# Both cross attentions: scores and row maxima two and a half units ahead in place of three, and the split of the maxima at the end of GpSimd's turn

## The reference, cut to what matters

```
scores = q k^T * scale            # 512 x 512 a head
p      = softmax(scores, axis=-1)
out    = p v                      # channels x 512
x      = layernorm(x + project(out))   # the second one has no projection
```

## Time and profile before

| | us |
|---|---|
| median of three runs | 3492.27 |
| lowest and highest | 3489.34, 3504.04 |
| the profiled execution's own time | 3488.51 |
| its span, first to last instruction | 3486.6 |
| c0, first row maximum to the last normalized batch | 525.67 to 943 |
| c1, the same | 2249.07 to 2932 |
| granted clock of PE, mean of the span | 0.939 |

### The profile page before, as it was taken

How to read it: one execution, slowest core, us unless ns; L and a number is a source line. 1 busy time by engine, 2 the same in 40 slices (tenths; PEclk the granted TensorE clock), 3 DMA queues, 4 the chain that set the end, 5 groups by cost and what they waited for, 6 DMA issues and landing times. The chain is left out here.

```text
span 3486.6 us, 57867 instructions
## 1 busy us (share of the span) xinstructions
PE 3037.0 (87%) x21948; PEld 1766.3 (51%) x21948; DVE 2121.2 (61%) x2636; ACT 1542.6 (44%) x2674; POOL 929.9 (27%) x1329
## 2 busy tenths in 40 slices
PE   7999968999579958999996999589999995889997
PEld 4444323333256636888885676222222222767785
DVE  4555658999335543444444344699999992572167
ACT  2222214777433213333331333179999994421132
POOL 3344451333200001111120245423333331001154
PEclk9999987999879988999997999789999997999998
DMA  3122335554221014454443122323333333339976
GB/s 114 58 80 74 89 98 124 155 161 136 98 84 33 9 37 130 128 160 153 124 151 100 52 89 77 114 83 100 113 111 106 106 94 99 99 115 360 396 246 181
DMA packets 374902, 421.67 MB, mean 121 GB/s; under 512 B 63249, under 2 KB 247185, under 8 KB 373394
## 3 DMA queue, kind: packets, MB, share of 16 engines
q1 hardware_dynamic: 216160, 260.08, 23.8%
q10 hardware_dynamic: 135938, 100.69, 9.4%
q0 software_dynamic: 22528, 57.19, 5.4%
HBM read 299.88 MB, written 117.31 MB: 120 GB/s over the span
## 5 line engine op out<-in xcount | busy, mean ns | idle before, releaser
L378 ACT ACTIVATE c_probs<-c_st 128x512 f32<-128x512 f32 x1536 | 835.7, 598 | 219.1 <-PE c_st L306 206.9
L414 DVE TENSOR_REDUCE c_maxes<-c_s 128x2 f32<-128x1024 f32 x768 | 904.2, 1212 | 38.0 <-PE c_s L287 32.9
L323 PE MATMUL c_o<-c_probs,c_v_aug 128*32 128x256 f32 x6144 | 495.6, 394 | 65.1 <-ACT c_o_raw L385 52.1
L287 PE MATMUL c_s<-c_k_st,c_q_st 48*128 48x512 bf16 (+1 forms) x1536 | 343.8, 445 | 71.2 <-DMA c_bo<-in_c_bo 25.3
L306 PE MATMUL c_st<-c_q_st,c_k_st 51*128 51x512 bf16 (+1 forms) x1536 | 318.7, 393 | 4.5 <-DVE c_y L439 4.3
L287 PEld LDWEIGHTS c_s<-c_k_st,c_q_st 48*128 48x128 bf16 (+1 forms) x1536 | 100.5, 128 | 402.5 <-issue 261.3
L323 PEld LDWEIGHTS c_o<-c_probs,c_v_aug 128*32 128x32 f32 x6144 | 124.3, 108 | 332.4 <-issue 226.1
L2916 DVE TENSOR_TENSOR f_w_lo<-f_w_raw,f_w_hi 128x1536 fp32r<-128x1536 f32 x64 | 116.8, 1825 | 107.8 <-ACT f_w_hi L2837 107.7
L306 PEld LDWEIGHTS c_st<-c_q_st,c_k_st 51*128 51x128 bf16 (+1 forms) x1536 | 145.4, 127 | 53.8 <-issue 21.5
L2837 ACT ACTIVATE f_w_hi<-f_w_raw 128x1536 fp32r<-128x1536 f32 x64 | 95.2, 1488 | 91.9 <-PE f_out_ps L2788 58.3
L2982 POOL CAST f_parts<-f_ctx 128x512 bf16<-128x512 f32 x16 | 13.7, 854 | 449.7 <-DMA f_ctx<-in_ctx 449.7
(11 more groups left out here) (418 smaller groups left out, 6026.9 us busy)
## 6 DMA issues: line engine op xcount, KB each, us to landing
c_o_dram<-c_o_raw SPq DMA_DIRECT2D x96, 256.0 KB, 2.5
f_w_raw<-in_f_win ACTq DMA_DIRECT2D x96, 256.0 KB, 3.0
f_w_raw<-in_f_wup ACTq DMA_DIRECT2D x96, 256.0 KB, 3.3
f_w_raw<-in_f_wdown ACTq DMA_DIRECT2D x96, 256.0 KB, 3.5
f_x<-x_dram SPq DMA_DIRECT2D x48, 256.0 KB, 3.8
c_k_dram<-f_parts ACTq DMA_DIRECT2D x96, 128.0 KB, 2.7
c_q_dram<-a_parts SPq DMA_DIRECT2D x96, 128.0 KB, 2.4
c_q_st<-c_q_dram SPq DMA_DIRECT2D x128, 96.0 KB, 2.2
```

What stands on the lines that cost most here:

```text
L287: mm = nc.tensor.matmul(s1_ps[:, i, half, :], q_st[r:r + ROWS, s, i, tt * P:(tt + 1) * P], k_st[r:r + ROWS, s, i, :], start=True, stop=True)
L323: mm = nc.tensor.matmul(o_ps[32 * h:32 * h + 32, queries], v_aug[:, (j // NG) % NBS, st, (j % NG) * G + h, :], probs[:, (st * 4 + i * 2 + ...
L378: nc.scalar.activation(probs[:, e % 8, :], st_ps[:, st_bank(j, e), :], ACT.Exp).then_inc(exp_done, 1)
L414: nc.vector.tensor_reduce(maxes[:, j % 2, :].rearrange("p (h r) -> p h r", h=2)[:, :, i * KT + tt], s1_ps[:, i, :, :], AX.X, ALU.max).then ...
```

## The change

The scores and row maxima run two and a half units ahead. The prologue does 20 slots in place of 24. In PE's and DVE's bodies the first four slots of a turn work on the second half of unit j+2 and the last four on the first half of unit j+3, which the new helper `slot_ahead` works out. `turn_max` of unit j+2 therefore stands in the middle of DVE's turn j, right behind its eighth slot, where it stood at the end of turn j-1. `split_max` of unit j+2 still belongs to POOL's turn j, but stands behind `place_v`, `normalize`, `gather_o`, `power`, `spread_recip` and `store_x` of that turn. In c1 only `normalize` still follows it. SP's and ACT's bodies stay as they are.

```diff
+        def slot_ahead(it, j, k):
+            n = (AHEAD - 1) * 2 * KT + KT + k
+            return it, j + n // (2 * KT), n % (2 * KT)
...
-                for j in range(AHEAD):
-                    for tt in range(KT):
-                        for i in range(2):
-                            scores(0, j, tt, i)
+                for n in range((AHEAD - 1) * 2 * KT + KT):
+                    scores(0, n // (2 * KT), n % (2 * KT) // 2, n % 2)
...
-                                if ahead:
-                                    scores(it, j + AHEAD, st, i)
+                                at, ahead, slot = slot_ahead(it, j, 2 * st + i)
+                                if unit_exists(ahead, last):
+                                    scores(at, ahead, slot // 2, slot % 2)
...
-                            if unit_exists(j + AHEAD, last):
-                                row_max(it, j + AHEAD, k // 2, k % 2)
+                            at, ahead, slot = slot_ahead(it, j, k)
+                            if unit_exists(ahead, last):
+                                row_max(at, ahead, slot // 2, slot % 2)
+                                if slot == 2 * KT - 1:
+                                    turn_max(at, ahead)
...
-                        if unit_exists(j + AHEAD, last):
-                            turn_max(it, j + AHEAD)
...
                         back_it, back_jb = batch_back(it, jb, LAG)
-                        if unit_exists(j + AHEAD - 1, last):
-                            split_max(it, j + AHEAD - 1)
                         if g == NG - 1 and not (last and jb == NBS - 1):
...
                         if g == 1 and normed:
                             store_x(b - 2, jb)
+                        if unit_exists(j + AHEAD - 1, last):
+                            split_max(it, j + AHEAD - 1)
```

More of the change, by code:

```diff
@@ L345, in body @@
                         b, jb, g, u = it * NBS + j // NG, j // NG, j % NG, it * RING + j
-                        ahead = unit_exists(j + AHEAD, last)
                         late = PROJ and to_load(first, jb, 2)
@@ L463, in _ @@
                 dve.wait_ge(const_ld, 16 * NCONST)
[L464 to L468, removed]
+                for n in range((AHEAD - 1) * 2 * KT + KT):
+                    row_max(0, n // (2 * KT), n % (2 * KT) // 2, n % 2)
+                    if n % (2 * KT) == 2 * KT - 1:
+                        turn_max(0, n // (2 * KT))
                 def body(it, first, last):
```

## The result

The changed kernel takes 3542.31 us (median of four runs, 3529.93 to 3549.65), the kernel before 3490.81. The ratio is 1.014, 95% interval 1.0115 to 1.0164: slower by 51 us where I forecast 14 more than before's median, and outside my range. The profiled execution took 3529.93 us, so between the two profiled ones 41.4 us are to be explained. It is the fastest of its four; the other three took 3540.65 to 3549.65 us at a mean granted clock of 0.922 to 0.925, where it had 0.930.

What follows compares the result with a forecast made beforehand. No engine had more than a few per cent to give, so only prologue and tail could shorten. 3488.5 - 6.4 (prologues) + 19.0 (c0's chain) = 3501.1, plus 3.8 for the median: 3505 us, range 3483 to 3528.

Steps and rivals of the forecast that it cites:

- Prologue: Start of both attentions: four slots fewer gain 4.1 us each, 8.2 in both, 6.4 after 1.8 for the clock.
- c1, steady: c1's bodies: sent maxima arrive with slack of 3.4 us, less 0.6, so c1 stays as it is, cost 0.
- c0, the chain: c0's split, send, store of o, gather, split, send: maxima late at g = 0 bodies, loss 19.0 us.
- six hops: Passes of c0's chain, each spanning two batches, batches 1 to 13: late by 1.5 us, then five times 3.5.
- S1: Zero point of c0's timeline: the moment PE's body of the unit with g = 1 starts.
- The first hop: c0's chain from batch 1 to 3, where store_x isn't there yet: 1.5 us late.
- Rival 3: c0's chain with L falling to 2.3: loss 13 us, total 3499, range 3493 to 3501; chance 0.20.
- L: Landing time of the split's DMA of c0's g = 1 turn, before SP starts the send; taken as 3.5 us.
- The other chain of a batch: c0, split of g = 1 to the next g = 1 body: ends at 22.5 us, needed at 23.25, just in time.
- rival 2: c0: late maxima also drop PE's clock, 2.6 us a drop, up to 3534, half dropping 3519; chance 0.25.

Runs made afterwards that it cites:

- e1: The changed kernel with split_max moved back to the start of POOL's turn in both attentions; ratio 1.019 to the kernel before.
- f1: The changed kernel with split_max at the start of POOL's turn in c0 and at its end in c1; 3486.11 us, ratio 0.9985.
- e3: The changed kernel with SP's store of o ahead of the loads of q and k in each turn; 3518.16 us, ratio 1.0084.
- e2: The kernel before, three units ahead, with only split_max moved to the end of POOL's turn; ratio 1.0185.
- f2: The changed kernel with split_max ahead of gather_o in c0's g = 0 turns, still at the end in g = 1 turns; ratio 1.006.
- f3: The kernel before with six idle waits in PE's c0 queue, each for a 256 KB DMA nothing else needs; 3545.45 us, ratio 1.0137.
- f4: The kernel before with twelve extra copies of a slot's score matmuls in six g = 0 bodies of c0; 3507.06 us, ratio 1.0041.
- e4: The changed kernel with ten extra copies of a pair of score matmuls ahead of six g = 0 bodies of c0; 3537.83 us, ratio 1.0128.

## Why the prediction was wrong, point by point

*Prologue.* Right. c1 is 4.5 us shorter (forecast 3.2 to 4.1); over all profiled executions with a c1 free of waits it takes 682.4 us on average with three units (four kernels) and 678.3 with two and a half (six), 4.1 less. c0 without waits is 7.2 (e1) and 9.2 us (f1) shorter, of which the clock's earlier rise is a part: 12.6 and 8.2 us at half clock in place of 21.3. At an equal clock 3.9 us are left (405.7 against 401.8). That rise isn't the change's doing as far as these runs tell: the first stretch at half clock lasts from 8.2 us (f1) to 32.1 (e3) with two and a half units, and from 10.6 (e2) to 21.3 with three. So the forecast's charge of 0.9 us a prologue for it is neither borne out nor refuted.

*c1, steady.* Right: no wait for sent maxima and 678.2 us. That it would be right for both positions of the split was never claimed, and e1 shows that it would not have been.

*c0, the chain.* Right in its mechanism, its place (g = 0 bodies, every second batch, six hops from batch 1 to 13) and nearly in its size: 21.5 us of waits against 19.0. Within the hop shown, the send to the store took 6.60 us as forecast; the landing of the split behind the gather took 726.98 - 723.10 = 3.9 us where I took 2.6 (it is the longest of them; their median is 2.4); the split's DMA of the g = 1 turn stood at 15.32 from S1 in place of 14.60; the store's way to the gather was 3.07, not 3.55. The first hop was late by 2.4, not 1.5. The errors are of both signs, as are the other five waits about the 3.5 I took, so that the sum came near is in part luck. Rival 3, an L of 2.3, didn't come: the least was 2.7.

*The other chain of a batch.* "Just in time" held in the changed kernel: no g = 1 body waits. It was tight: with 14.6 and 4.4 us as forecast and the L of 2.7 to 5.7 us read at the hops it ends 21.7 to 24.7 us behind S1, with 23.25 at hand, by my estimate; the longer batches gave it room, as the prediction says. In f2 it was late, by a write that was 3 us longer there.

*The clock.* This is the step that failed. The forecast's sum had no term for it; it stood as rival 2, at a chance of 0.25 and with 2.6 us for each drop, half of them dropping. All six waits dropped it. The price came from one stretch of 6.8 us, which I took for the length of every drop. The six lasted 17.0, 17.0, 13.6, 13.6, 6.7 and 6.7 us. The excess over before of 90.1 - 21.3 = 68.8 us at half clock costs 0.43 each, 29.6 us (25 at f3's 0.36): more than the waits. The sum 414.2 - 4.1 + 21.5 + 29.6 = 461 stands beside the measured 458.4. With that term the forecast would have been some 3535, inside the measured runs, and outside my range, which ended at 3528 because I gave this case only half its price.

That rival 2's upper end, 3534, comes so near is luck of two errors. It had 11 late bodies, where the prediction's own chain has six, and 2.6 us a drop, where the six cost about 5 us each (75 us at half clock, at 0.4). With six drops it would have said 3521. The rows to see that waits drop the clock were there: it had fallen behind an idle stretch of 2.8 us elsewhere, and my own waits were 3.5. That a drop can outlast 6.8 us though PE is busy, the rows could have told me too: behind c0's prologue PE was busy for 10.00 of 10 us at 0.50.

The Trainium skill, TensorE: Matmul & The Clock Gate (HAM oscillation — how this bites in real kernels), tells of a loop that waits for a DMA each round and starts each round's work at the low clock. The traces agree: 0.81 to 0.91 granted where PE idles, 1.00 where matmuls stand in the same places (f3 and f4). I should have put it among the terms.

## What to carry to other kernels

An engine that is moved closer to its producer must be followed through the in-order queues of the engines in between: here nothing waited on the maxima themselves, but a send that waits stood ahead of a store, a gather waited for that store, and the next split stood behind the gather. A new wait of 2 us or more on a TensorE that is otherwise full is to be priced with its clock, which cost here about 1.4 times the waits in the changed kernel and 1.6 times in f3. A term taken out of such a chain can come back in another, as in e3, where the loads left the chain and stood right ahead of its next write. And one order for two instances of a function is two changes: look at each instance's order by itself.

## What was not expected of the hardware

The granted clock fell with waits as short as 1.3 us (f2, at 787.2) in the midst of dense work. Between the first and the last `scores_t` of c0, over all kernels here, PE waited 23 times for 2 us or more, and the clock fell every time; it waited 16 times for 1 to 2 us, and the clock fell with eight of these, while it stayed at 1.00 with one of 1.86 us (e4). It then stayed at 0.50 for 3.4 (f2) to 41 us with PE busy for nearly all of the time behind the wait: 17.00 of 17 us at 617.4 in after, 40.78 of 41 at 734.4 in e3. Before's c0 began in the same way, at 0.50 for 21.3 us with PE full, and c1 got its clock after 8. Which of these lengths a wait gets is open.

The same write of 16 KB on POOL's queue landed in 5.0 to 6.9 us in f2's batches between 600 and 840, and in 1.8 to 3.3 in the changed kernel's; the split's write of 64 KB took a median of 4.6 us in e3 and 2.4 in the changed kernel. Both differ by what SP issues just ahead of them; which transfers hold them up wasn't looked into.
